# First attention: queries and keys projected once per batch and taken from DRAM, against projected once per unit in the stacks' layout

## What is computed

```
qkv = (h @ w_qkv + b_qkv).reshape(B, T, 3, NUM_HEADS, HEAD_DIM)
qkv = jnp.transpose(qkv, (2, 0, 3, 1, 4))
q, k, v = (qkv[0], qkv[1], qkv[2])
scores = jnp.einsum('bhqd,bhkd->bhqk', q, k) / np.sqrt(HEAD_DIM)
attn = jax.nn.softmax(scores, axis=-1)
out = jnp.einsum('bhqk,bhkd->bhqd', attn, v)
```

## Time and profile before

| | us |
|---|---|
| median of 3 runs | 2901.57 |
| lowest and highest | 2901.55, 2903.66 |
| the profiled execution | 2903.02 |
| its span in the profile | 2901.2 |

### The profile page before, as it was taken

How to read it: one execution, slowest core, us unless ns; L and a number is a source line. 1 busy time by engine, 2 the same in 40 slices (tenths; PEclk the granted TensorE clock), 3 DMA queues, 4 the chain that set the end, 5 groups by cost and what they waited for, 6 DMA issues and landing times.

```text
span 2901.2 us, 46560 instructions
## 1 busy us (share of the span) xinstructions
PE 2730.1 (94%) x16447; PEld 2034.3 (70%) x16447; DVE 2304.3 (79%) x4143; ACT 2099.3 (72%) x4664; POOL 1800.3 (62%) x1357
## 2 busy tenths in 40 slices
PE   6999999999899999999999999999999999999996
PEld 3333333333357777788888888988888888888885
DVE  8888989898947887788777778777777787777776
ACT  2787887877766555677777777777777787777773
POOL 3442534422025555677788778788778787778873
PEclk6899999999999999999999999999999999999997
DMA  1000000000022210000000000000000000000000
GB/s 41 7 7 7 12 7 7 7 7 2 2 78 77 86 39 30 8 1 1 1 1 3 3 1 3 3 1 3 3 1 3 3 1 3 3 1 3 3 3 6
DMA packets 25689, 34.83 MB, mean 12 GB/s; under 512 B 4136, under 2 KB 14952, under 8 KB 25456
## 3 DMA queue, kind: packets, MB, share of 16 engines
q1 hardware_dynamic: 25456, 31.85, 3.5%
HBM read 29.08 MB, written 2.23 MB: 11 GB/s over the span
## 4 chain that ended last, share of the span: by engine, by line
PE 67%; DVE 13%; ACT 10%; POOL 5%; issue 5%; DMA 0%; DVEq 0%; POOLq 0%; ACTq 0%
PE P L1828 17%; PE P L1853 11%; PE P L1696 8%; PE P L1839 5%; PE P L1757 5%; PE P L1658 4%; PE P L1670 4%; PE P L1862 3%; DVE a_mx L1241 3%; ACT a_PT L799 3%; PE P L1768 2%; PE P L1811 2%; PE P L1648 2%; DVE c_nm L1396 2%; ACT c_P L929 2%
## 5 line engine op out<-in xcount | busy, mean ns | idle before, releaser
L1396 DVE TENSOR_REDUCE c_nm<-P 128x1 f32<-128x1024 f32 x512 | 623.7, 1218 | 171.5 <-PE P L1828 171.1
L1241 DVE TENSOR_REDUCE a_mx<-P 128x1 f32<-128x512 f32 x1024 | 638.1, 682 | 84.7 <-PE P L1658 82.0
L929 ACT ACTIVATE c_P<-P,c_nm 128x1024 f32<-128x1024 f32 x512 | 575.6, 1124 | 132.4 <-DVE c_nm L1396 132.1
L2075 POOL TENSOR_TENSOR c_P<-c_P,c_P 128x1024 f32<-128x1024 f32 (+1 forms) x256 | 622.3, 2431 | 21.3
L799 ACT ACTIVATE a_PT<-P 128x512 f32<-128x512 f32 x968 | 503.2, 605 | 112.2 <-PE P L1670 111.0
L2073 POOL TENSOR_SCALAR c_P<-c_P,c_rr 128x1024 f32<-128x1024 f32 (+1 forms) x256 | 304.1, 1188 | 305.8 <-DVE c_rr L1408 305.6
L1828 PE MATMUL P<-c_xth,c_Th 128*128 128x512 f32 x1024 | 367.2, 440 | 42.5 <-ACT c_P L929 42.3
L1853 PE MATMUL P<-c_DT,c_xkh 128*128 128x256 f32 x2048 | 393.6, 285 | 5.6 <-DVE c_xkl L1388 5.0
L1670 PE MATMUL P<-a_Qs,a_Ks 32*128 32x512 f32 x968 | 325.8, 487 | 42.7 <-ACT a_PT L799 36.4
L1421 DVE TENSOR_TENSOR c_DT<-P,c_DT 128x512 fp32r<-128x512 f32 x512 | 348.4, 681 | 12.5 <-ACT c_DT L940 11.7
L1853 PEld LDWEIGHTS P<-c_DT,c_xkh 128*128 128x128 f32 x2048 | 331.5, 193 | 6.6 <-DVE c_xkl L1388 5.6
(11 more groups left out here) (248 smaller groups left out, 5389.9 us busy)
## 6 DMA issues: line engine op xcount, KB each, us to landing
b_cwB<-cw_scratch SPq DMA_DIRECT2D x64, 256.0 KB, 5.0
c_stg<-in_cw SPq DMA_DIRECT2D x8, 640.0 KB, 3.9
a_Qs<-a_mT SPq DMA_DIRECT2D x256, 2.0 KB
b_stg<-in_moe SPq DMA_DIRECT2D x9, 384.0 KB, 3.1
out<-xres SPq DMA_DIRECT2D x15, 128.0 KB, 1.8
xres<-in_x SPq DMA_DIRECT2D x3, 512.0 KB, 8.1
xres<-in_x SPq DMA_DIRECT2D x2, 256.0 KB, 3.0
a_hTl_f<-in_wqk SPq DMA_DIRECT2D x1, 512.0 KB, 4.0
```

Source lines behind the costliest of these rows:

```text
L929: e.activation(m.P1[s][n % 4][:, :], P[:, k:k + 2, :].rearrange("p c k -> p (c k)"), ACT.Exp, bias=m.nm[:, n % 4, s:s + 1], accum_out=m.sm ...
L1241: e.tensor_reduce(m.mx2[u % 2][:, t // 4, j, t % 4, half:half + 1], bank("maxima", u, t, j, half), AX, ALU.max).then_inc(m.S["a_max_dve"])
L1396: e.tensor_reduce(m.nm[:, n % 4, s:s + 1], P[:, k:k + 2, :].rearrange("p c k -> p (c k)"), AX, ALU.max, negate=True).then_inc(m.S["c_nm"])
L2075: e.tensor_tensor(p0, p0, p1, ALU.add).then_inc(m.S["c_D"])
```

## The change

Queries and keys are projected once for a batch and half, with all 16 heads in one 128x128 weight (`project(b, wh, c)`: b from 0 to 3 in place of u from 0 to 15). ACT adds the bias and rounds to the high part `m.nh`, DVE makes the low part `m.nl` from the same bank of PSUM in one SCALAR_TENSOR_TENSOR. `keep_heads(b, wh, c)` writes them with three DMAs of 256 KB (high part twice, low part once) into a DRAM tensor `qk_scratch` of the form [2, 16 heads, 4, 8, T], which has the stacks' layout. Its fourth rows are filled once, zeros for Q and ones for K, by two DMAs of 512 KB. `spread_heads(u, wh, c)` brings a half stack with one DMA of 256 KB. The rows of maxima go by two DMAs of four rows each in place of eight of one row.

The steps `project` after the first batch stand where those of units 4, 8 and 12 stood, so that of the 30 pairs of the loop 6 remain: the pairs that project the keys and the queries of units 4, 8 and 12 stay as those of batches 1, 2 and 3, and the pairs of the other twelve units go. All projections of batch 0 stand ahead of the first maxima.

```diff
@@ SIGNALS, READ
-    "project": project_signals,
+    "project": {"a_qk_pe": 1, "a_nh": 1, "a_nl": 1},
+    "spread_heads": lambda u, wh, c: {f"a_stack{u % 3}_{c}": 16},
+    "keep_heads": lambda b, wh, c: {f"a_qk{c}": 48},
-    "project": lambda *a: [("a_tq", "project", *a)],
+    "project": lambda *a: [("a_nl", "project", *a)],
@@ plan_all
-    put(("project", 0, 1, 0))
-    put(("project", 0, 0, 0))
-    put(("turn_h", 0, 1))
-    hook(0, 4, "project", 0, 1, 1)
-    hook(1, 2, "project", 0, 0, 1)
+    for c in range(2):
+        if c:
+            put(("turn_h", 0, 1))
+        for wh in (1, 0):
+            put(("project", 0, wh, c))
+            p.do("keep_heads", 0, wh, c)
+        for wh in (1, 0):
+            p.do("spread_heads", 0, wh, c)
...
-                hook(s0 + 3 - w, 1, "project", u + 1, w, c)
+                if gr == 3:
+                    hook(s0 + 3 - w, 1, "project", b + 1, w, c)
+                    hook(s0 + 4 - w, 0, "keep_heads", b + 1, w, c)
+                hook(s0 + 5 if gr == 3 else s0 + 2, 0, "spread_heads", u + 1, w, c)
@@ ACT
+    def project(b, wh, c):
+        w.wait_ge(*at("a_qk_pe", "project", b, wh, c))
+        if b:
+            w.wait_ge(*at(f"a_qk{c}", "keep_heads", b - 1, 0, c))
+        e.activation(m.nh[wh][:, 512 * c:512 * c + 512], bank("project", b, wh, c), ACT.Identity,
+                     bias=m.bqk[:, wh:wh + 1]).then_inc(m.S["a_nh"])
@@ DVE
+    def project(b, wh, c):
+        cs = slice(512 * c, 512 * c + 512)
+        w.wait_ge(*at("a_nh", "project", b, wh, c))
+        e.scalar_tensor_tensor(out=m.nl[wh][:, cs], in0=bank("project", b, wh, c), scalar=m.bqk[:, wh:wh + 1],
+                               in1=m.nh[wh][:, cs].bitcast(F32), op0=ALU.add,
+                               op1=ALU.subtract).then_inc(m.S["a_nl"])
@@ PE maxima
+        w.wait_ge(*at(f"a_stack{u % 3}_{half}", "spread_heads", u, 0, half))
+        w.wait_ge(*at(f"a_stack{u % 3}_{t // 4}", "spread_heads", u, 0, t // 4))
@@ SP
+    def keep_heads(b, wh, c):
+        cs = slice(512 * c, 512 * c + 512)
+        if b:
+            for u in range(4 * b - 4, 4 * b):
+                w.wait_ge(*at(f"a_stack{u % 3}_{c}", "spread_heads", u, 0, c))
+        w.wait_ge(*at("a_nh", "project", b, wh, c))
+        for r in range(2):
+            e.dma_start(m.qk[wh, :, 2 * r if r and not wh else r, :, cs], m.nh[wh][:, cs].bitcast(F32)).then_inc(
+                S[f"a_qk{c}"], 16)
+        w.wait_ge(*at("a_nl", "project", b, wh, c))
+        e.dma_start(m.qk[wh, :, 2 if wh else 1, :, cs], m.nl[wh][:, cs].bitcast(F32)).then_inc(S[f"a_qk{c}"], 16)
+    def spread_heads(u, wh, c):
+        b, gr = divmod(u, 4)
+        cs = slice(512 * c, 512 * c + 512)
+        w.wait_ge("a_one", 32)
+        w.wait_ge(*at(f"a_qk{c}", "keep_heads", b, 0, c))
+        if u > 2:
+            w.wait_ge(*at("a_st", "scores", u - 3, 15, 1))
+        e.dma_start((m.Ks if wh else m.Qs)[u % 3][:, cs].bitcast(F32),
+                    m.qk[wh, 4 * gr:4 * gr + 4, :, :, cs].rearrange("h r d k -> (h r d) k")).then_inc(
+                        S[f"a_stack{u % 3}_{c}"], 16)
     def row2_low(u, c):
...
-        for j in range(4):
-            for r in range(2):
-                row = 32 * j + 24 + r
-                e.dma_start(m.Qs[u % 3][row:row + 1, 512 * c:512 * c + 512].bitcast(F32).rearrange(
-                    "p (t q) -> p t q", t=4), m.mT[u % 2][c][4 * j:4 * j + 4, r, :].bitcast(F32)).then_inc(
-                        S[f"a_mdma{u % 3}_{c}"], 16)
+        for r in range(2):
+            e.dma_start(m.Qs[u % 3][24 + r:128:32, 512 * c:512 * c + 512].bitcast(F32).rearrange(
+                "p (t q) -> p t q", t=4), m.mT[u % 2][c][:, r, :].bitcast(F32)).then_inc(S[f"a_mdma{u % 3}_{c}"], 16)
```

More of the change, by code:

```diff
@@ L146 @@
 }
-def project_signals(u, w, c):
-    out = {"a_qk_pe": 1, "a_tq": 1}
-    if u == 0 and (w == 1 or c == 0):
-        out |= {"a_first_dve": 3}
-    else:
-        out |= {"a_th": 2, "a_qs": 1}
-    return out
 def snapped(on_dve):
@@ L603, in memory @@
     m.PT = sb("a_PT", [128, 4, 4, 512])
+    m.zero, m.one = [put(f"a_fill{i}", [128, T], F32, where[m.PT.name][2] + 4096 * i) for i in range(2)]
+    m.two = sb("a_two", [128, 1])
     m.Vp = [sb(f"a_Vp{i}", [128, NT * 144 + 32]) for i in range(2)]
-    m.tq = [sb(f"a_tq{i}", [128, 512]) for i in range(2)]
-    m.th = [sb(f"a_th{i}", [128, 512]) for i in range(2)]
     m.OT = sb("a_OT", [128, T])
@@ L719, in a_early_free @@
 def a_early_free(v):
-    return [v.at("a_st", "scores", 14, 15, 1), v.at("a_qk_pe", "project", 15, 0, 1),
+    return [v.at("a_st", "scores", 14, 15, 1), v.at("a_qk0", "keep_heads", 3, 0, 0), v.at("a_qk1", "keep_heads", 3, 0, 1),
             v.at("a_v_dve", "values", 3, 1), v.at("a_xn", "residual", 3), v.at("a_hT_pe", "turn_h", 3, 1)]
@@ L774, in turn_h @@
                          scale=m.gb[:, 0:1]).then_inc(m.S["a_hT_act"])
-    def project(u, wh, c):
-        gr, k = u % 4, projects.index((u, wh, c))
-        w.wait_ge(*at("a_qk_pe", "project", u, wh, c))
-        if k > 1:
-            uu, ww, cc = projects[k - 2]
-            w.wait_ge(*at("a_first_dve" if uu == 0 and (ww, cc) != (0, 1) else "a_qs", "project", uu, ww, cc))
-        e.activation(m.tq[k % 2][:, :], bank("project", u, wh, c), ACT.Identity,
-                     bias=m.bqk[:, wh, gr:gr + 1]).then_inc(m.S["a_tq"])
-    projects = [s[1:] for s in v.plan.steps if s[0] == "project"]
+    def project(b, wh, c):
[4 more added lines that the diff above has]
+                     bias=m.bqk[:, wh:wh + 1]).then_inc(m.S["a_nh"])
     def row2(u, c):
@@ L1639, in values, with project @@
         tt.then_inc(m.S["a_v_pe"])
-    def project(u, wh, c):
-        b, gr = divmod(u, 4)
-        ps = bank("project", u, wh, c)
+    def project(b, wh, c):
+        ps = bank("project", b, wh, c)
         cs = slice(512 * c, 512 * c + 512)
@@ L1963, in one @@
     def one(i):
-        w.wait_ge(*v.now("a_qs", "one", i))
         e.memset(m.Vp[i][:, :], 1.0).then_inc(m.S["a_z"])
     def first():
+        e.memset(m.zero[:, :], 0.0).then_inc(m.S["a_fill"])
         for h, done in ((0, 9), (1, 18), (0, 30), (1, 45)):
@@ L1972, in first @@
             e.tensor_tensor(m.rs[:, c], m.ve[:, c], m.mh[:, c], ALU.pow).then_inc(m.S["a_first_pool"])
+        w.wait_ge("a_two", 1)
+        w.wait_ge("a_fill", 1)
+        e.tensor_scalar(m.one[:, :], m.zero[:, :], m.two[:, 0:1], 0.0, ALU.add, ALU.add).then_inc(m.S["a_fill"])
     def ln_gather(who, b, k):
@@ L2226, in build @@
         m.P8 = ctx.enter_context(nc.psum_tensor("P", [128, 8, 512], F32))
-        names = ["id", "mh", "a_w", "b_w", *[f"x{b}" for b in range(B + 1)], *v.end]
+        names = ["id", "mh", "a_fill", "a_two", "a_one", "a_w", "b_w", *[f"x{b}" for b in range(B + 1)], *v.end]
         m.S = {n: ctx.enter_context(nc.semaphore(n)) for n in dict.fromkeys(names)}
```

102 lines of the change are left out of this document (39 added, 63 removed).

## The result

The changed kernel takes 2866.91 us at the median of four runs (2861.42 to 2875.01), the kernel before 2901.56 (2898.46 to 2903.66): a ratio of 0.988, 95% interval 0.985 to 0.992, so 34.7 us or 1.2% faster. The forecast was 2879, its range 2866 to 2906. The profiled executions are 2903.02 and 2872.34, 30.7 us apart, where the prediction's sum had 22.3.

The account below looks back on a forecast made before the run. TensorE, 94% busy, was taken as the bound, with VectorE and ScalarE near it. Terms -34.0 + 2.9 + 4.8 + 2 + 2 = -22.3 took 2903.0 to 2880.7, less 1.45 excess: 2879; range 2866 to 2906.

Parts of the forecast that it names:

- Removed pairs: Attention loop: ten units lose two pairs each, 1.70 us apiece on TensorE's path; 34.0 us less.
- The pairs that stay: Six kept pairs: banks become free after VectorE's a_nl instead of ScalarE's copy, 0.8 each; 4.8 us more, between 0 and 9.
- VectorE as the next limit: Stretches with the next batch's layer norm: VectorE nearly bounds them once pairs go; 2 us more, between 0 and 6.
- The start: Before the first scores: maxima about 7 us late through DRAM, mostly regained without projections between them; 2 us more taken.
- The estimate by the Trainium skill: Start: about 2 us fixed cost per DMA and DRAM the heaviest target; start would be 1 us worse.
- The slow clock: After the first sums: the 1.2 GHz level lasts until full-width turns raise it; 2.9 us more than before.
- I take the first `divide`: Slot 12, nine rounds after the first sums: its turns raise the clock, 2.9 us more; chance 0.58.
- early rise: Rival: the clock rises with the first sums, ten rounds at 2.64; 14 less, 2865; chance 0.07.
- the second `divide`: Rival: slot 16 raises the clock, not the first `divide`; eight more slow rounds, +11.6, 2891; chance 0.15.
- The slower rival: Clock stays at 0.50 until the pair in slot 26, 36 slow rounds; 42 more, 2921; chance 0.09.
- the last two: Rivals: clock falls after kept pairs, 2903 to 2915, chance 0.05; or stacks land late in every unit, held excluded.
- The third `divide`: Rival: only the third divide after the first sums raises the clock; 2902; chance 0.06.

Follow-up runs that it names:

- ghost: Changed kernel with the six matmuls of each of the 24 removed pairs put back, result unused, without ScalarE copies and GpSimd passes; 2906.76 us, ratio 1.002.
- fills: Changed kernel with the constant ones written first by GpSimd and the scratch fills issued ahead of the later three batches' loads of x; 2878.0 us, ratio 0.992.
- fills2: The kernel of fills, unchanged, run once more for the spread; 2866.81 us, ratio 0.990.
- four: The kernel of both with four unused 128x128 transposes in place of the six unused matmuls; times 2859.51 to 2865.25 us, ratio 0.986.
- again2: Changed kernel, nothing edited, another repeat with a profile; 2868.94 us (2863.29 to 2877.07), ratio 0.990.
- late: Changed kernel with the first divide of unit 0 moved from slot 12 to slot 16; 2866.96 us, ratio 0.990.
- rows: Kernel before with one part of the change alone, the rows of maxima in two DMAs per unit; 2898.93 us, ratio 1.000.
- again: Changed kernel, nothing edited, run once more with a profile; 2865.01 us at the median of six (2861.58 to 2890.23), ratio 0.990.
- warm: Changed kernel with six unused full-width matmuls of the projection's form behind the first sums, in round 0; 2864.98 us, ratio 0.988.
- both: Changed kernel with the earlier fills of fills and the six unused matmuls of warm; times 2860.91 to 2863.11 us, ratio 0.987.
- both7: The kernel of both with the unused matmuls one slot earlier, among the last maxima before the first scores; times 2859.40 to 2868.52 us, ratio 0.987.
- cap: Changed kernel with six unused projection-form matmuls in round 4 of unit 0, where the kernel before had its first pair; 2871.01 us, ratio 0.989.

## Why the prediction was right, and where it was not

**Removed pairs: right.** 34.0 predicted, 33.9 in the profile; ghost shows that 1.58 of the 1.70 a pair are PE's own time.

**The pairs that stay: right in kind, too large.** 4.8 was predicted from 0.8 a pair. Scores do wait for VectorE's a_nl, as said, but only 0.31 longer a round, and the round of a `divide` behind the second pair is 0.25 longer: 6 x 0.31 + 3 x 0.25 = 2.6. I took each bank's delay whole; in the timeline above waits of 0.45 and 0.18 us lengthen the round by only 0.3.

**VectorE as the next limit: nothing.** Unit 4, with a layer norm beside it, lasts 44.84; before it was 48.17, and less 3.40 it would be 44.77. The 11.5 of 11.7 us that the earlier trace rows left was no bound; that the norms' work finds room in the rounds around is my reading and not shown. I had taken 2.

**The start: right, in part by errors that cancel.** Maxima at 31.7 (31 predicted), scores at 67.5 (68), cost 1.1 (2 taken). But ten units of 0.78 to 0.95 from 16 on end at 23.8 to 25.5 and not at 25 to 27; they ended at 24.5. And from the last store's issue to the first read 3.2 us passed (24.52 to 27.72), where the prediction had 1.2 from the earlier trace rows. The estimate by the Trainium skill that stands beside it is worked out from a figure for DMAs issued by GpSimd; here SyncE issued them.

**The slow clock: right for the execution that was profiled, wrong as a rule.** The step that failed is "I take the first `divide`", with 0.58 against 0.07 for an early rise, and behind it the sentence that only a change of the start could bring the early one "since the rows show the contrary". The rows showed one execution. The term itself held in the profiled one: the eleventh sums start 40.10 behind the first, 2.1 more than before, where 2.9 was predicted. Where the clock goes up in the fourteen profiles (in fills, fills2 and four the level ahead of it is read from the length of the sums):

| kernel | clock up at | round | full-width work there |
|---|---|---|---|
| again2, late | 76.9, 77.1 | 0 | none |
| rows, again | 80.1, 81.2 | 1 | the small turn of the maxima, 1.5 ahead |
| ghost | 92.7 | 3 | none |
| warm, both, both7 | 79.3, 74.6, 72.3 | 0, 0, before 0 | unused pair |
| four | 80.5 | 1 | unused transposes in round 0 |
| before, cap | 92.7, 94.4 | 4 | a pair |
| after, fills2 | 109.9, 108.7 | 8 | turns of the first divide |
| fills | 145.1 | 17 | turns of the second, in round 16 |

Two things happen. In two of the three profiles of the changed kernel, and by their times in about half of its executions, the clock rises within the first rounds, on scores, maxima and sums, with at most the small turn. In the others it stays down longer, and all five profiled rises later than round 3 lie in full-width work or at most 2.3 us behind it. The 2870.67 of late warns against making a rule of this. The forecast described the slower kind well and gave the first 7%; nine of sixteen were of it. The early case was priced at 14 less than the first-divide case; the last sums of again2 and after are 10.8 apart, since in again2 the rise comes 3.2 us behind the start of the first sums and not with it. For the second `divide` I had 2891; the slowest execution took 2890.2, which fits by its time. The median is 12 below the forecast by both errors. The profiled execution is 8.4 below the 2880.7 of the sum (kept pairs 2.2, VectorE 2, the start 0.9, the slow clock 0.7, the end 2.7), and half of the executions lie some 9 lower again. That the median of 2866.91 fell inside the range from 2866 on is luck: it lies 0.9 inside, between two heaps, and again, the same kernel, has its median at 2865.01.

The Trainium skill says in "TensorE: Matmul & The Clock Gate", section "What's actually happening", that throttled is the default and that matmul activity releases the clock. The profiles agree in part: scores, maxima and sums at 4.71 busy of 5 us (with the small turn in two cases) released it in rounds 0 to 3 in five of them, and did not over eight rounds in after and over sixteen in fills.

**The tail and the rest: 2.7 that I had not seen.** 0.9 in the last two units, 1.8 behind them. In the parts that follow, which the change doesn't touch, the clock drops for some 3 us at a time, as here in after:

```profile
1543.60:1546.80 3.20, 3.20 (x10) 0.50 0.00 0
1547.00:1550.00 3.00, 3.00 (x26) 1.00 0.00 0
```

Fills and ghost have five such drops between 840 and 2600, after seven, before and rows eight, again nine; the time of the execution behind the start of the last sums is 2067.1 and 2067.0, 2069.0, 2070.8 and 2070.4, and 2072.3. So the 1.8 go with one drop fewer, and again, the changed kernel too, takes longer here than before did: it isn't an effect of the change.

**The slower rival** (low until slot 26, 2921) has no execution in these runs. Neither have the last two: in after the clock stays up from 109.9 to 765.2, and behind unit 0 no maxima wait for a DMA. The third `divide` was reached in one run out of ten of fills at most, by its time.

**Open.** What makes an execution one kind or the other isn't shown. From the first maxima to 76 us again2 and after have the same instructions within 0.3 us; what differs ahead of that is when the clock goes up and down in the start (up at 18.9 and 24.6). No run shifts the rounds in small steps at the start, which might tell whether the rise depends on how they lie to these moments. The counts (9 of 16, 15 of 16) are small.

## What to carry to other kernels

Work on the busiest engine comes off one for one when nothing else waits last: here 1.70 us for each pair, foreseen from two rows. But ask what else the removed work did. If wide matmuls go from a stretch of matmuls over 32 rows or columns, TensorE's clock may stay low for longer in some executions: six unused wide ones right behind the first sums cost under 3 us, and the eight times of warm and both lie within 4.8 us, where the sixteen without them spread over 29. And a single profile shows one execution; where the times of a kernel stand in two heaps, profile it until there is one of each before a rule is read from it.

## What I had not expected of the hardware

- The same program on the same data rose to the fast clock at 76.9, 81.2 or 109.9, and its time was 2863.3, 2865.6 or 2872.3. The kernel before rose at 92.7 and rows, which differs from it only in DMAs, at 80.1.
- Rounds with PE busy for 4.71 of 5 us stayed on the slow clock for seventeen rounds, 145.1 - 72.0 = 73 us, in fills, with eight full-width transposes among them (the level read from sums of 1.94 us).
- The drops of some 3 us in the later parts, five to nine between 840 and 2600 us, go with up to 5 us of the 2870, more than the differences between the best versions here.
